# Attention output kept by features, its softmax sums inverted on VectorE, and integers transposed in bfloat16

## The chip, the cores and the metric

One NeuronCore of a Trainium2 chip runs the kernel. The metric is the device time of one execution in microseconds (us). TensorE (PE in the profile) multiplies; its weight loads stand apart as PEld. VectorE (DVE), ScalarE (ACT) and GpSimd (POOL) work on tiles; SyncE (SP) issues most DMAs.

## The reference

Input x has 8 batches of 512 tokens by 256 features. Per batch:

```python
x = layernorm(x * s1)                      # s1, s2: halves of the condition
q, k, v = x @ Wq.T, x @ Wk.T, x @ Wv.T     # each output column scaled (demodulation)
v = v * s2
out = softmax(q k.T / 4) v                 # 16 heads of 16 features
y = (out @ Ww.T) * w_dc + (v @ Wu.T) * u_dc
# int8 feed-forward: rows of y and columns of rhs scaled by their absolute maximum
res = x_in + round(y / s_y) @ round(rhs / s_r) * s_y * s_r
```

## The kernel before

The batches follow one another as t = 0 to 7. One batch is 16 rounds: 4 groups of 4 heads, and 4 tiles of 128 keys each. A round has two units, each of two score products (heads in the lower and the upper 64 rows of the array) and one exponential of 128x1024 on ScalarE (L529). The score banks are double-buffered: unit u waits for the exponential of unit u-2. Two rounds make one of the 8 stretches (`SUPER`) of a batch: `scores_of(r)`, `values_of` of the two rounds before, `scores_of(r+1)`, then `fill(t, i)`, which holds the rest of TensorE's work (L1401 to L1409). In what follows a = t+1 is the batch being prepared, z = t-1 and y = t-2 the batches being finished.

The value product `values_of` (L1037) uses four column groups of 32: 16 columns of a head's values, then ones, so that rows 16 to 31 of each group of 32 hold the softmax sum. Four heads fill `o_acc` (128x512). `save_o` (L537, ScalarE) copies it to `o_t` after each of the four groups of heads, between the exponentials; the next group's values wait for the copy (`o_saved`).

From there the attention output is brought to natural layout and back: `to_natural` (four 128x128 transposes per group of heads), `normalise` on VectorE (L732 inverts the sums, L733 multiplies, into `o_nat`), `to_features` (two times four transposes per batch), `output_features` on VectorE (L748), and the product with the weights, `output` (L1162). VectorE adds the skip and quantises (`quantise`, L760 to L770); TensorE transposes the rounded float32 values (`quantised_transposed`); VectorE subtracts the rounding constant into bfloat16 (`integers`, L774); TensorE multiplies (`int_product`, L1202); VectorE scales (`product`, L790); GpSimd adds the residual (L418) and stores.

The same loop prepares batch a: VectorE multiplies x by the style (`modulate`, L617), measures it (`measure`, L623 to L629) and normalises it; TensorE transposes x; VectorE splits it into a high and a low part (`features`, L610 and L611); TensorE forms q and k (`projected`, L1065); ScalarE copies the high part of each (`high_part`, L513) and VectorE the low part (`low_part`, L650 and L653); DMAs on SP's queue gather both into the stacks. The skip matrix (L1076, "fold"), the norms of q and k for a bound on the scores (`norms`, `largest_norms` L681, `norms_transposed`, `bound_flag`) and the values (L1088) follow. `row_maxima` on TensorE and `row_shift` on VectorE read the flag; with these inputs both take the short branch.

Order and coupling: each engine runs its list in order. `step_fills` writes by hand in which order TensorE's fills claim the three `work` banks; use n waits until use n-3 is freed by its reader, almost always VectorE (`work_freed`), and VectorE takes the banks in the same order (`ready`). VectorE's order is the list at L918 to L986. In it `norms_transposed` of stretch 7 needs `largest_norms(a)`, which stands behind everything that VectorE does for that batch from the fourth low part on:

```python
low_part(a, 3)                 # L963
quantise(z, 0); product(y, 1); normalise(t, 1); skip_matrix(a)
measure(); integers(z, 0); quantise(z, 1)
largest_norms(a); bound_flag(a); v_and_skip(a, 0)
```

TensorE's fills before, in stretches 0 to 7 of a full batch: v1, v2, `to_natural`(z,3) | v3, x transposed twice | `to_features`(z,0), q0, k0 | `to_features`(z,1), `to_natural`(t,0), q1 | integer product (y,0), k1, `output`(z,0) | integer product (y,1), `to_natural`(t,1), fold | `quantised_transposed`(z,0), `output`(z,1), norms | `norms_transposed`, v0 of a, `to_natural`(t,2), `quantised_transposed`(z,1), flag.

After the last value product the rest of batch 7 runs alone: copy, transposes, inverse, transposes, output product, quantisation, integer product, residual, store (L1418 to L1429).

Of the kernel before, what the change touches and what calls it, by code (L numbers as in the profile page):

```python
# [13 lines left out]
P = 128  # L14
# [18 lines left out]
def step_fills(t, last):  # L33

    a, z, y = t + 1, t - 1, t - 2
    if t == 0:
        return [[("row", 0, 0), ("row", 0, 1), ("v", t, 0), ("v", t, 1), ("v", t, 2)],
                [("v", t, 3), ("xt", a, 0), ("xt", a, 1)],
                [("q", a, 0), ("k", a, 0)],
                [("on", t, 0), ("rhs", 0, 0), ("q", a, 1)],  # L40
                [("k", a, 1)],
                [("on", t, 1), ("fold", a, 0), ("rhs", 0, 1)],
                [("norms", a, 0)],
                [("v", a, 0), ("on", t, 2), ("rhs", 0, 2)]]
    if t == last:
        return [[("v", t, 1), ("v", t, 2), ("on", z, 3)],
                [("v", t, 3), ("ot", z, 0), ("ot", z, 1)],
                [("ffn", y, 0), ("y", z, 0)],
                [("ffn", y, 1), ("on", t, 0), ("y", z, 1)],
                [("yqt", z, 0), ("on", t, 1)],  # L50
                [("yqt", z, 1), ("first features", t, 0)],
                [("ffn", z, 0), ("ffn", z, 1), ("y", t, 0), ("y", t, 1)],
                [("on", t, 2)]]
    ffn = [[("ffn", y, n)] if y >= 0 else [] for n in range(2)]
    return [[("v", t, 1), ("v", t, 2), ("on", z, 3)],
            [("v", t, 3), ("xt", a, 0), ("xt", a, 1)],
            [("ot", z, 0), ("q", a, 0), ("k", a, 0)],
            [("ot", z, 1), ("on", t, 0), ("q", a, 1)],
            ffn[0] + [("k", a, 1), ("y", z, 0)],
            ffn[1] + [("on", t, 1), ("fold", a, 0)],  # L60
            [("yqt", z, 0), ("y", z, 1), ("norms", a, 0)],
            [("v", a, 0), ("on", t, 2), ("yqt", z, 1)]]


def adaln_ffn_kernel(nc, x, cond, wq, wk, wv, ww, wu, rhs, out):
# [38 lines left out]
    with ctx:  # L104
# [55 lines left out]
        o_t = sb("o_t", [P, G, S])  # L160
# [7 lines left out]
        inv_den = sb("inv_den", [P, KT, 4])  # L168
        o_nat = sb("o_nat", [P, KT, H])

        o_t2 = sb("o_t2", [P, 2, HC, S // 2])
        y_q = o_t2[:, :, :, :].rearrange("p i c t -> p (i c t)").rearrange("p (k o) -> p k o", k=KT)
# [5 lines left out]
        demod_rows = o_nat[:, :, :].rearrange("p k h -> p (k h)")[0:B, 0:3 * H].rearrange(  # L178
            "b (m o) -> b m o", m=3)
        y_qt = sb("y_qt", [P, HC, S], BF16)  # L180


        by_two = [o_t2[:, :, :, :].rearrange("p m c t -> p (m c t)").rearrange("p (m c i) -> p m c i", m=2, c=HC),
# [1270 lines left out]
```

## Time and profile before

| | us |
|---|---|
| median of 3 runs | 452.48 (452.22 to 453.28) |
| the profiled execution | 452.78 |
| its span, first to last instruction | 451.0 |
| granted TensorE clock, mean | 0.973 of 2.4 GHz |
| busy: PE, DVE, ACT, POOL | 427.1, 245.3, 294.8, 107.2 |

A busy time is a sum over the whole span; it does not tell what waits for what. The chain of waits follows the work that ended last back from its end. The timeline gives each engine's instructions with the idle time before them and what ended it (the releaser). Float32 products on TensorE stand as two records each in the counts. Successive records of an engine can overlap by a few hundredths of a microsecond.

### The profile page before, as it was taken

The numbers are of one execution on the slowest core, as the hardware profiler recorded it, in microseconds if no ns is written. First come the engines' busy times: TensorE is split into PE (matmuls) and PEld (weight loads), VectorE is DVE, ScalarE is ACT, GpSimd is POOL, SyncE is SP. The second block draws the span as 40 slices with busy tenths as digits, with TensorE's granted clock in tenths as the row PEclk, the third lists the DMA queues.
The fourth block names the chain that finished last, engine by engine and source line by source line (L and its number), as shares of the span: only waits on it lengthen the run. The fifth ranks groups of instructions, "written<-read, shape, count | busy, mean of one in ns | idle before, by whom it ended". The sixth has DMA issues, their size and how long they took to land.

```text
span 451.0 us, 7767 instructions
## 1 busy us (share of the span) xinstructions
PE 427.1 (95%) x2700; PEld 238.9 (53%) x2700; DVE 245.3 (54%) x566; ACT 294.8 (65%) x343; POOL 107.2 (24%) x114
## 2 busy tenths in 40 slices
PE   8986999899999999899999999999999999999975
PEld 7773555355545555455544555455545555554444
DVE  6645546544575447644675557654674555537225
ACT  3433488768775787567775776768667776578731
POOL 7176111301130124202340123202330123002201
PEclk9596899999999999999999999999999999999989
DMA  4399179505961299217941499218951399102021
GB/s 155 106 133 135 17 172 137 71 4 156 136 85 55 101 145 152 70 41 157 148 86 55 123 132 156 65 37 163 134 89 56 80 139 146 48 0 95 1 93 47
DMA packets 29326, 44.19 MB, mean 98 GB/s; under 512 B 3880, under 2 KB 15144, under 8 KB 29256
## 3 DMA queue, kind: packets, MB, share of 16 engines
q1 hardware_dynamic: 27040, 38.31, 49.3%
q0 software_dynamic: 1040, 3.70, 2.5%
q10 hardware_dynamic: 1200, 1.59, 2.3%
q8 instruction: 26, 0.43, 0.4%
q14 instruction: 20, 0.16, 0.2%
HBM read 14.17 MB, written 4.25 MB: 41 GB/s over the span
## 4 chain that ended last, share of the span: by engine, by line
PE 84%; DVE 7%; issue 2%; DMA 2%; ACT 2%; SPq 1%; POOL 0%; DVEq 0%; POOLq 0%
PE o_acc L1037 23%; PE scores L1023 16%; PE work L1088 11%; PE work L1065 9%; PE work L1000 8%; PE work L1162 5%; PE work L1076 3%; DMA k_stack<-parts 2%; PE work L1202 2%; ACT probs L529 2%; PE work L1334 1%; PE work L1176 1%; DVE o_t L767 1%; SPq L266 1%; DVE o_t L760 1%
## 5 line engine op out<-in xcount | busy, mean ns | idle before, releaser
L529 ACT ACTIVATE probs<-scores 128x1024 f32<-128x1024 f32 x256 | 247.8, 1024 | 101.7 <-PE scores L1023 101.7
L1037 PE MATMUL o_acc<-probs,v_aug 128*32 128x512 f32 x1024 | 123.3, 598 | 0.2 <-ACT probs L529 0.2
L1023 PE MATMUL scores<-q_stack,k_stack 50*128 50x512 f32 x512 | 95.7, 448 | 7.6 <-ACT probs L529 2.7
L410 POOL TENSOR_TENSOR squares<-parts 128x512 bf16<-128x512 f32 x30 | 31.3, 1042 | 219.3 <-ACT parts L513 219.3
L1023 PEld LDWEIGHTS scores<-q_stack,k_stack 50*128 50x128 f32 x512 | 39.2, 185 | 79.7 <-ACT probs L529 58.7
L1037 PEld LDWEIGHTS o_acc<-probs,v_aug 128*32 128x32 f32 x1024 | 26.6, 109 | 61.6 <-issue 56.7
L1088 PE MATMUL work<-vs_w,x_t 128*128 128x512 f32 x192 | 53.1, 421 | 0.0
L1065 PE MATMUL work<-x_t,qk_w 128*128 128x512 f32 x168 | 44.5, 406 | 0.2 <-DVEq L642 0.2
L1088 PEld LDWEIGHTS work<-vs_w,x_t 128*128 128x128 f32 x192 | 35.9, 197 | 13.4 <-issue 6.1
L671 DVE TENSOR_TENSOR v_aug<-work,rows 128x256 f32<-128x256 f32 x32 | 13.6, 425 | 47.5 <-PE work L1088 47.5
L418 POOL TENSOR_TENSOR res<-res,x_res 128x512 f32<-128x512 f32 x15 | 19.1, 1276 | 74.1 <-DVEq L796 74.1
L1065 PEld LDWEIGHTS work<-x_t,qk_w 128*128 128x128 f32 x168 | 30.0, 188 | 7.1 <-issue 0.6
L1000 PE MATMUL work<-ident,o_t 128*128 128x128 f32 x180 | 26.5, 276 | 0.0
L1162 PE MATMUL work<-w_demod,o_t 128*128 128x256 f32 x112 | 26.5, 379 | 0.0
L1000 PEld LDWEIGHTS work<-ident,o_t 128*128 128x128 f32 x180 | 20.7, 140 | 6.4 <-issue 4.0
L537 ACT ACTIVATE o_t<-o_acc 128x512 f32<-128x512 f32 x32 | 19.2, 599 | 6.1 <-PE o_acc L1037 5.9
L1162 PEld LDWEIGHTS work<-w_demod,o_t 128*128 128x128 f32 x112 | 20.6, 190 | 2.7
L790 DVE SCALAR_TENSOR_TENSOR res<-work,y_scale,rhs_scale_row 128x256 f32<-128x256 f32 x28 | 12.3, 479 | 15.3 <-PE work L1202 15.0
L653 DVE SCALAR_TENSOR_TENSOR parts<-work,cols,parts 128x512 fp32r<-128x512 f32 x14 | 10.5, 750 | 17.7 <-ACT parts L513 17.7
L748 DVE COPY o_t<-work 128x512 f32<-128x512 f32 x14 | 9.7, 692 | 18.6 <-PE work L1000 18.2
L760 DVE TENSOR_TENSOR o_t<-work,skip 128x512 f32<-128x512 f32 x16 | 11.1, 691 | 12.0 <-PE work L1162 8.9
L650 DVE TENSOR_TENSOR parts<-work,parts 128x512 fp32r<-128x512 f32 x14 | 9.7, 692 | 12.4 <-ACT parts L513 12.4
(158 smaller groups left out, 434.5 us busy)
## 6 DMA issues: line engine op xcount, KB each, us to landing
q_stack<-parts SPq DMA_DIRECT2D x96, 128.0 KB, 6.3
k_stack<-parts SPq DMA_DIRECT2D x88, 128.0 KB, 7.7
x_res<-in_x_dram SPq DMA_DIRECT2D x8, 512.0 KB, 4.5
x_sb<-in_x_dram SPq DMA_DIRECT2D x7, 512.0 KB, 3.6
out_dram<-res POOLq DMA_DIRECT2D x7, 512.0 KB, 6.3
rows<-rows_dram SPq DMA_DIRECT2D x7, 384.0 KB, 3.3
rows<-in_cond_dram SPq DMA_DIRECT2D x8, 128.0 KB, 3.7
k_stack<-parts ACTq DMA_DIRECT2D x8, 128.0 KB, 9.9
```

The source lines that it names most:

```text
L410: nc.gpsimd.tensor_tensor(squares[:, n, :], parts[:, n, 0, :], parts[:, n, 0, :], ALU.mult).then_inc(squares_ready, 1)
L418: nc.gpsimd.tensor_tensor(res[:, two, :], res[:, two, :], x_res[:, two, :], ALU.add).then_inc(res_added, 1)
L529: nc.scalar.activation(probs[:, r % RING, pair:pair + 2, :], scores[:, pair:pair + 2, :], ACT.Exp).then_inc(exp_done, 1)
L537: nc.scalar.activation(o_t[:, group % G, :], o_acc[:, :], ACT.Copy).then_inc(o_saved, 1)
L671: nc.vector.tensor_tensor(v_aug[:, k, :, 0:D], both[:, 0:H].rearrange("p (h d) -> p h d", d=D), rows[:, 1, :].rearrange("p (h d) -> p h d" ...
L760: link(nc.vector.tensor_tensor(y, bank.rearrange("p (k o) -> p k o", k=2), skip[:, z % 2, two, :], ALU.add))
L1000: return nc.tensor.transpose(dst, src, ident[0:rows, 0:rows])
L1023: last = nc.tensor.matmul(scores[:, 2 * (u % 2) + e, :], k_stack[top:top + ROWS, t % 2, 2 * g + u % 2, kt * P:(kt + 1) * P], q_stack[top:t ...
L1037: last = nc.tensor.matmul(o_acc[DV * j:DV * (j + 1), :], v_aug[:, kt, 4 * g + j, :], probs[:, r % RING, j, :], start=(kt == 0), stop=(kt = ...
L1065: last = nc.tensor.matmul(bank, lhs, right, start=(n == 0), stop=(n == len(operands) - 1))
L1088: last = nc.tensor.matmul(bank, lhs, right, start=(n == 0), stop=(n == len(operands) - 1))
L1162: last = nc.tensor.matmul(bank[:, k * H:(k + 1) * H], o_t2[:, i, c, k * P:(k + 1) * P], w_demod[:, z % 2, c, :], start=(c == 0), stop=(c = ...
```

## The change

- The value columns of odd groups of heads move to the second 16 of each 32 (`v_aug`, now written by two VectorE instructions), and the heads are regrouped so that the two groups of a pair fill all 128 rows, in the order of the features.
- ScalarE copies the first group of a pair twice, once with a mask for the value rows (`o_raw`) and once for the sum rows (`den`). VectorE adds the second group to both (`add_second`), straight from `o_acc`.
- `invert`: 32x32 block transposition of `den`, two reciprocals, and a block transposition back; `normalise` multiplies 128x512. The result `o_n` is by features, so `output` reads it directly. `to_natural`, `to_features` and `output_features` are gone.
- `quantise` (but for the last batch) writes integers in bfloat16 (`y_int`), which TensorE multiplies by a bfloat16 identity; `integers` clips at -127.
- Fills and VectorE's list are reordered; `quantise` is split into `add_skip` and `quantise`.
- At the end, 12 products of ones by the identity stand in the place of the transposes.

TensorE's fills after: v1, v2 | v3, x transposed twice | q0, k0 | `output`(z,0), `output`(z,1) | q1, k1 | integer product (y,0), fold | integer product (y,1), `quantised_transposed`(z,0), norms | `norms_transposed`, v0 of a, `quantised_transposed`(z,1), flag.

```diff
@@ POOL, start
+            pool.wait_ge(const_ready, 1)
+            nc.gpsimd.tensor_copy(ident_b[:, :], ident[:, :]).then_inc(unit_ready, 1)
@@ ACT
-            def save_o(group):
-                act.wait_ge(pv_done, KT * (group + 1))
-                if group >= G:
-                    act.wait_ge(work_ready, USE[("on", group // G - 1, group % G)] + 1)
-                nc.scalar.activation(o_t[:, group % G, :], o_acc[:, :], ACT.Copy).then_inc(o_saved, 1)
+            def save_first(pair):
+                act.wait_ge(pv_done, KT * (2 * pair + 1))
+                if pair > 0:
+                    act.wait_ge(o_normed, pair)
+                nc.scalar.activation(o_raw[:, :], o_acc[:, :], ACT.Copy, scale=in_half[:, 0:1])
+                nc.scalar.activation(den[:, :], o_acc[:, :], ACT.Copy, scale=in_half[:, 1:2]).then_inc(o_saved, 1)
...
-                    if i == 0 and t > 0:
-                        save_o(t * G - 1)
-                    if i in (2, 4, 6):
-                        save_o(t * G + i // 2 - 1)
+                    if i in (2, 6):
+                        save_first(2 * t + i // 4)
...
-                        if i == 3:
+                        if i == 4:
                             high_part(a, 2)
-                        if i == 4:
                             high_part(a, 3)
@@ DVE, v_and_skip
-                nc.vector.tensor_tensor(v_aug[:, k, :, 0:D], both[:, 0:H].rearrange("p (h d) -> p h d", d=D),
-                                        rows[:, 1, :].rearrange("p (h d) -> p h d", d=D), ALU.mult)
+                by_pair = "p (n j e d) -> p n j e d"
+                for e in range(2):
+                    nc.vector.tensor_tensor(
+                        v_aug[:, k, :, e * D:(e + 1) * D].rearrange("p (n e j) d -> p n e j d", e=2, j=4)[:, :, e, :, :],
+                        both[:, 0:H].rearrange(by_pair, e=2, j=4, d=D)[:, :, :, e, :],
+                        rows[:, 1, :].rearrange(by_pair, e=2, j=4, d=D)[:, :, :, e, :], ALU.mult)
@@ DVE, in place of normalise(z, g), first_chunk and output_features
+            def add_second(pair):
+                dve.wait_ge(pv_done, KT * (2 * pair + 2))
+                dve.wait_ge(o_saved, 2 * pair + 1)
+                nc.vector.scalar_tensor_tensor(den[:, :], o_acc[:, :], in_half[:, 0:1], den[:, :], ALU.mult, ALU.add
+                                               ).then_inc(den_ready, 1)
+                nc.vector.scalar_tensor_tensor(o_raw[:, :], o_acc[:, :], in_half[:, 1:2], o_raw[:, :], ALU.mult, ALU.add
+                                               ).then_inc(o_saved, 1)
+            def invert(pair):
+                dve.wait_ge(den_ready, pair + 1)
+                link(nc.vector.transpose(den_t[:, :], den[:, :]))
+                by_half = den_t[:, :].rearrange("p (b e d) -> p b e d", e=2, d=D)
+                for e in range(2):
+                    last = nc.vector.reciprocal(inv_den[:, :, 1 - e], by_half[:, :, e, 0])
+                link(last)
+                link(nc.vector.transpose(inv_t[:, :].rearrange("p (b e d) -> p b e d", e=2, d=D),
+                                         inv_den[:, :, :].unsqueeze(3).broadcast_to([P, S // DV, 2, D])))
+            def normalise(pair):
+                dve.wait_ge(o_saved, 2 * pair + 2)
+                if pair < 2 * B - 1:
+                    nc.vector.tensor_tensor(o_n[:, pair % 2, :], o_raw[:, :], inv_t[:, :], ALU.mult).then_inc(o_normed, 1)
+                else:
+                    for i in range(2):
+                        tokens = slice(i * HALF_S, (i + 1) * HALF_S)
+                        nc.vector.tensor_tensor(o_n[:, pair % 2, tokens], o_raw[:, tokens], inv_t[:, tokens], ALU.mult
+                                                ).then_inc(last_normed, 1)
@@ DVE, quantise
+                if z < B - 1:
+                    for k in range(2):
+                        last = nc.vector.tensor_scalar(y_q[:, 2 * i + k, :], y[:, k, :], y_inv[:, 2 * i + k:2 * i + k + 1],
+                                                       MAGIC, ALU.mult, ALU.add)
+                    link(last)
+                    nc.vector.tensor_scalar(y_int[:, two, :], y, MAGIC, INT8_MAX, ALU.subtract, ALU.min
+                                            ).then_inc(yq_ready, 1)
+                    return
@@ DVE, start
+            for e in range(2):
+                link(nc.vector.tensor_reduce(in_half[:, e:e + 1], ident[:, :].rearrange("p (j e d) -> p j e d", e=2, d=D)[:, :, e, :],
+                                             AX.XY, ALU.add))
+            dve.sem_inc(half_ready, 1)
@@ PE, quantised_transposed
-                    transpose_pair(claim("yqt", z, i), y_q, i, work_ready)
+                    bank = claim("yqt", z, i)
+                    for c in range(HC):
+                        for k in range(2):
+                            last = nc.tensor.matmul(bank[:, (2 * c + k) * P:(2 * c + k + 1) * P],
+                                                    y_int[:, 2 * i + k, c * P:(c + 1) * P], ident_b[:, :],
+                                                    start=True, stop=True)
+                    last.then_inc(work_ready, 1)
@@ PE, end
-            to_natural(z, 3)
-            pe.wait_ge(on_ready, z * G + G)
-            one_chunk(scores[:, 1, :], 1).then_inc(features_t, 1)
+            keep_clock(scores[:, 0, :], 12)
```

VectorE's list for a full batch, after the change:

```python
add_second(2*z + 1); v_and_skip(t, 1); v_and_skip(t, 2)
invert(2*z + 1); normalise(2*z + 1); v_and_skip(t, 3)
features(a, 0); features(a, 1); low_part(a, 0); low_part(a, 1)
add_skip(z, 0); add_skip(z, 1); add_second(2*t); low_part(a, 2); low_part(a, 3)
invert(2*t); normalise(2*t); quantise(z, 0); product(y, 0); skip_matrix(a)
modulate(a + 1); measure(); quantise(z, 1); product(y, 1); integers(z, 0)
largest_norms(a); bound_flag(a); v_and_skip(a, 0); integers(z, 1)
row_shift(a); normalise_x(a + 1)
```

## Rows read from the trace of the kernel before

**Rows 1.** Part 1 of the page: busy us (share of the span) xinstructions
```profile
PE 427.1 (95%) x2700; PEld 238.9 (53%) x2700; DVE 245.3 (54%) x566; ACT 294.8 (65%) x343; POOL 107.2 (24%) x114
```

**Rows 2.** Chain of waits, 225 to 240 us: start, duration, what
```profile
225.42 0.66 PE scores L1023 x4
226.08 1.85 PE o_acc L1037 x16
...
229.19 1.74 PE work L1162 x8
...
230.95 0.70 DVE o_t L760
...
236.94 0.87 PE work L1000 x8
```

**Rows 3.** TensorE's timeline: start, duration, operation [idle before, releaser]
```profile
216.15 1.64 PE L1065 MATMUL work<-x_t,qk_w 128*128 128x512 f32 x6
...
235.21 0.27 PE L1000 MATMUL work<-ident,norm_max 128*1 128x128 f32 x1 [0.78 <-DVE norm_max L681]
...
253.62 0.65 PE L1000 MATMUL work<-ident,o_nat 128*128 128x128 f32 x4
```

**Rows 4.** Windows: length, busy (instructions) by engine, clock, DMA, GB/s
```profile
88.65:137.98 49.33, 48.17 (x309) 25.66 (x310) 27.38 (x65) 35.25 (x40) 8.48 (x9) 1.00 0.54 88
188.12:238.16 50.04, 48.91 (x317) 26.34 (x318) 29.16 (x67) 35.35 (x40) 11.84 (x12) 1.00 0.59 107
338.17:387.54 49.37, 48.93 (x317) 26.34 (x318) 25.43 (x57) 35.34 (x40) 8.93 (x9) 1.00 0.59 96
387.54:433.06 45.52, 44.49 (x302) 21.35 (x302) 18.70 (x44) 32.77 (x36) 6.62 (x6) 1.00 0.18 59
```

**Rows 5.** Groups by line and form: busy us, mean ns, idle before
```profile
L1202 PE MATMUL work<-rhs_q,y_qt 128*128 128x256 bf16 x56 | 8.4, 275 | 0.0
...
L732 DVE RECIPROCAL inv_den<-work 128x16 f32<-128x16 f32 x31 | 8.0, 258 | 14.6 <-PE work L1000 9.4 <-DVE res L790 1.5 <-DVE o_t L748 1.5
```

**Rows 6.** VectorE's timeline, a full batch
```profile
214.48 1.23 DVE L617 TENSOR_TENSOR x_sb<-x_sb,rows 128x1024 f32<-128x1024 f32 x1 [0.22 <-DVE parts L653]
...
218.54 0.69 DVE L650 TENSOR_TENSOR parts<-work,parts 128x512 fp32r<-128x512 f32 x1 [1.12 <-ACT parts L513]
...
220.40 0.69 DVE L763 TENSOR_REDUCE amax<-o_t 128x2 f32<-128x512 f32 x1 [0.15 <-DVE o_t L760]
...
222.18 0.43 DVE L770 TENSOR_SCALAR o_t<-o_t 128x512 f32<-128x512 f32 x1
223.29 0.88 DVE L790 SCALAR_TENSOR_TENSOR res<-work,y_scale,rhs_scale_row 128x256 f32<-128x256 f32 x2 [0.68 <-PE work L1202]
...
227.12 1.41 DVE L623 BATCH_NORM_STATS2 stats<-x_sb 128x6 f32<-128x256 f32 x4 [0.24 <-DVE vs_w L611]
...
229.22 0.69 DVE L774 TENSOR_SCALAR y_qt<-work 128x512 bf16<-128x512 f32 x1
...
249.66 0.43 DVE L671 TENSOR_TENSOR v_aug<-work,rows 128x256 f32<-128x256 f32 x1 [3.59 <-PE work L1088]
...
252.95 0.69 DVE L611 TENSOR_TENSOR x_t<-work,x_t 128x512 fp32r<-128x512 f32 x1
```

**Rows 7.** Chain of waits, 430 to 440 us
```profile
433.08 0.61 ACT o_t L537
...
436.38 3.52 PE work L1176 x8
```

**Rows 8.** ScalarE's timeline, batch 7
```profile
419.12 3.77 ACT L529 ACTIVATE probs<-scores 128x1024 f32<-128x1024 f32 x4 [1.04 <-PE scores L1023]
```

**Rows 9.** Windows around idle TensorE; the clock stands behind POOL's time
```profile
34.00:36.00 2.00, 0.06 (x1) 0.00 (x0) 1.20 (x2) 0.04 (x1) 2.00 (x2) 1.00 1.08 128
36.00:38.00 2.00, 0.73 (x4) 0.33 (x4) 0.58 (x2) 0.87 (x1) 2.00 (x1) 0.83 1.05 125
...
437.00:439.00 2.00, 2.00 (x6) 1.55 (x6) 0.74 (x2) 0.00 (x0) 0.00 (x0) 0.50 0.00 0
```

More of the change, by code:

```diff
@@ L966, in _ @@
                 if y >= 0:
-                    product(y, 1)
-                normalise(t, 1)
+                    product(y, 0)
                 skip_matrix(a)
@@ L972, in _ @@
                 if a + 1 < B:
+                    modulate(a + 1)
                     measure()
                 if z >= 0:
+                    quantise(z, 1)
+                if y >= 0:
+                    product(y, 1)
+                if z >= 0:
                     integers(z, 0)
-                    quantise(z, 1)
                 largest_norms(a)
@@ L979, in _ @@
                 v_and_skip(a, 0)
-                normalise(t, 2)
                 if t == 0:
@@ L987, in _ @@
                     normalise_x(a + 1)
-            normalise(B - 1, 3)
-            quantise(B - 1, 0)
-            quantise(B - 1, 1)
+            add_second(2 * B - 1)
+            invert(2 * B - 1)
+            normalise(2 * B - 1)
+            for i in range(2):
+                add_skip(B - 1, i)
+                quantise(B - 1, i)
             product(B - 1, 0)
@@ L1130, in row_maxima @@
                 pe.nop()
-            def to_natural(z, g):
-                pe.wait_ge(o_saved, z * G + g + 1)
-                if (z, g) == (B - 1, G - 1):
-                    bank, done = scores[:, 0, :], natural_t
-                else:
-                    bank, done = claim("on", z, g), work_ready
-                for q in range(KT):
-                    last = transpose(bank[:, q * P:(q + 1) * P], o_t[:, g, q * P:(q + 1) * P])
-                last.then_inc(done, 1)
             def transpose_pair(bank, src, i, done):
@@ L1300, in fill @@
                         int_product(z, 1)
+                    else:
+                        if y >= 0:
+                            int_product(y, 1)
+                        if not first:
+                            quantised_transposed(z, 0)
+                        norms(a)
+                else:
+                    if last:
                         last_output(t, 0, 0)
@@ L1303, in fill @@
                     else:
-                        if not first:
-                            quantised_transposed(z, 0)
-                            output(z, 1)
-                        norms(a)
-                else:
-                    if last:
-                        to_natural(t, 2)
-                    else:
                         norms_transposed(a)
                         values(a, 0)
-                        to_natural(t, 2)
                         if first:
```

218 lines of the change are left out of this document (91 added, 127 removed).

## The prediction

> **What bounds the kernel now.** I read the busy shares first: TensorE is busy 95% of the span, ScalarE 65%, VectorE 54% [rows 1]. That says that TensorE's work counts, not that it alone sets the time. So I read the chain that ended last through a batch [rows 2]: it runs along TensorE (scores, values, fills), and behind the last output product (229.19) it leaves it for VectorE, where the skip is added at 230.95. It comes back with `norms_transposed` at 235.21, for which TensorE had idled 0.78 us, released by `norm_max` [rows 3]. One VectorE chain per batch is thus already on the path.
>
> Then the batches by stretches between their first score products [rows 4]. Call them 0 to 7: batch 1 takes 49.33 us, batches 2 to 5 50.05 each (137.98 to 338.17), batch 6 49.37, batch 7 45.52 up to the last value product. The granted clock is 1.00 in all. I cut a full batch at two points. A: from its first scores (188.12) to the end of the second k projection (216.15 + 1.64 = 217.8) [rows 3], 29.7. B: from there over VectorE to `norms_transposed`, 235.2, 17.4. C: to the next batch's scores, 238.16, 2.95.
>
> **A, TensorE's part.** Eight transposes take 0.87 in the chain [rows 2], so a group of four is 0.44. The change takes four such groups out of A (two of `to_natural`, two of `to_features`): 1.76. The integer product moves behind the k projection: 8.4 us for 14 of them is 0.6 [rows 5]. Both output products now stand ahead of it, 1.74 each [rows 2]: +3.5. One wait is new. The last `v_and_skip` starts at 249.66 and the second low part of x ends at 252.95 + 0.69 = 253.64 [rows 6], while TensorE was free at 253.62 and covered the hand-over with transposes [rows 3]. Those are gone, and `v_and_skip` has one instruction more (about 0.13), so the q projection waits some 0.35. A becomes 29.7 - 1.8 - 0.6 + 3.5 + 0.35 = 31.1.
>
> **B, VectorE's part, in the new order.** `low_part(3)` ends 1.43 after the k projection (217.80 to 218.54 + 0.69) [rows 6]; with 0.22 for the semaphores behind it, 1.65. Everything after it is now queued back to back:
> - `invert` and `normalise`. The block transpose is in no row. Bounds: 0.43, the cheapest 128x512 float32 SBUF step (222.18), and 1.23, the 128x1024 one (214.48). I take 0.69, what plain 128x512 steps take (229.22) [rows 6], since it moves 512 elements a row once. Two reciprocals of 16 columns at 0.26 [rows 5] overlap to 0.45, links 0.1, the multiplication 0.69: 0.69 x 2 + 0.45 + 0.1 + 0.69 = 2.6.
> - `quantise(0)` without its addition: 220.40 to 222.61, 2.2. `product(0)`: 0.88 and a link of 0.24, 1.1. `skip_matrix`: two of 0.69 and links, 1.65.
> - `modulate`, moved in from where it was hidden: 1.25. `measure`: 227.12 to 229.22, 2.1 [rows 6].
> - `quantise(1)` 2.2, `product(1)` 1.1, `integers` 0.9, the reduction 0.7.
>
> Sum: 1.65 + 2.6 + 2.2 + 1.1 + 1.65 + 1.25 + 2.1 + 2.2 + 1.1 + 0.9 + 0.7 = 17.5. It was 17.4: the two additions left, and so did waits for TensorE inside, but the inversion, `modulate` and one product came in.
>
> TensorE no longer has work for that time. Two of its eight stretches a batch lie there, then the scores and values of a third: 0.66 + 1.85 + 0.66 = 3.2 [rows 2]. The first stretch adds a product (0.6) and the fold, which like an output product is eight matrix passes of 256 columns (1.7): 5.5. The second adds only 1.3, so ScalarE stretches it to about 5.5: two copies of 0.6 [rows 7] stand between its exponentials. TensorE is at `norms_transposed` 5.5 + 5.5 + 3.2 = 14.2 us after the k projection and waits 3.2, where it waited 0.8. What transposes are saved behind A is thus worth nothing.
>
> **C.** 2.95, less a group of four transposes (0.44) and about 0.1 for the bfloat16 ones: 2.4. A full batch: 31.1 + 17.5 + 2.4 = 51.0, +0.95.
>
> Here I weigh a page. The Trainium skill (VectorE: DVE Perf Modes, The three transpose paths) gives 311 ns for a VectorE transposition of 128x128 bfloat16, in 32x32 blocks only. An estimate by four such pieces is 1.24 us an instruction, so 1.1 more for each `invert`; a full batch would be 52.1 by its chain alone. No row here shows one.
>
> **The sum.** Start and batch 0: two more reductions ahead of a VectorE memset and one more POOL copy, +0.2 (nothing to 0.8, since VectorE idles later anyway); two of batch 0's stretches lose their transposes or a projection, and ScalarE's exponentials and copies set them, while others keep their length: +0.9. Batch 1 has no integer products, so B is 15.3: 48.8, -0.5. Batches 2 to 5: +0.95 x 4 = +3.8. Batch 6 has no `modulate` or `measure` and B would be 14.1, so TensorE's 14.2 takes its place: 47.7, -1.6. Batch 7: fewer transposes, but ScalarE gives 3.77 of exponentials and idles 1.04 a stretch there already [rows 8], 4.8, and now holds most stretches: -0.5. Tail: from the last copy of values to the output products 3.3 us (433.08 to 436.38 [rows 7]); now two additions (1.45), the inversion (1.95) and half a multiplication, 3.95: +0.6. If the added fillers keep the clock up, the cold output products (3.52) get back 0.9 of that on the path: +0.1, between -0.3 and +0.6. Total +2.4: the profiled execution's 452.8 us becomes 455.2; the median of the runs stands 0.3 under it, 454.9.
>
> **The clock.** At 34 to 36 us TensorE is busy 0.06 of 2 us, and in the next 2 us the granted clock falls; at 437 to 439, behind the tail's copies, it is 0.50 (1.2 GHz) [rows 9]. The new wait of 3.2 looks like these, though it lies between dense stretches. In the tail the cold output products take 3.52 [rows 7] for what takes 1.74 hot, so a fall costs some 1.6 us. I take one in batches 2 to 5: 456.5. The Trainium skill (TensorE: Matmul & The Clock Gate, HAM oscillation) tells of a kernel whose bursts are parted by waits and that turns cold behind each. By that rule every full batch would pay.
>
> **Rivals.**
> - *Each long wait cools TensorE.* By the rows [rows 9], 4 x 1.6 = 6.4 us on 454.9, 461.3. Against it: batch 7's waits for ScalarE [rows 8] brought no fall, its clock is 1.00. 0.16.
> - *The chain is shorter (faster).* It decides where B falls below 16.85, 0.65 less than I sum: five batches then take 3.3 back, the 2.4 and 0.9 more. Two transposes at 0.43 give 0.5; if reciprocals and links overlap and q's wait vanishes too, 1.0 a batch: 454.9 - 5 = 450. The releaser of `norms_transposed` would stay VectorE. 0.24.
> - *TensorE stays the bound, as six groups of transposes a batch suggest.* 2.6 + 0.2 + the 0.8 wait is 3.6; over 7 batches 25, less some 6 that ScalarE's stretches give back: 434. It needs B under 14.2, against a sum of 17.5. 0.05.
> - *The transposition takes 1.2 us.* `invert` then also delays the last `v_and_skip`, where its slack is only 0.2 us, and so q: 6 x 2 more, 467. 0.06.
>
> **Numbers.** My forecast, the VectorE chain with a batch of 51 us, has 0.49; its own range is 451.5 to 459.5 (B half a microsecond either way in five batches, none to two falls), the likeliest time 456.5. Below 449.5 lies about 0.1, above 463 about 0.1. A measurement of this kernel tells 0.2%, 0.9 us, from no change. Faster: the shorter chain and the TensorE case, 0.29. Same: a part of the forecast near 452.5, 0.13. Slower: the rest, 0.58.
>
> **What would show it.** After the change: TensorE idle before `norms_transposed`, released by `norm_max`, about 3 us in batches 2 to 5, 1.5 in batch 1, near nothing in batch 6 (wrong if it is under 1 in the full ones). VectorE without a gap between the fourth low part and `norm_max`, 16 us. Batches of 51.0, 48.8 and 47.7. The transposition at 0.6 to 0.75. A granted clock under 1.00 behind one of the waits. TensorE's busy time down by some 20 us and the span not. The prediction is wrong at its root if the chain of waits never passes over VectorE between the projections and the norms.

## The result, and the profile after

The changed kernel takes 468.76 us (median of 4 runs, 466.3 to 470.45), the kernel before 452.35 beside it: a ratio of 1.036, with a 95% interval of 1.033 to 1.039. The prediction said 456.5, with an own range of 451.5 to 459.5 and about 0.1 each for below 449.5 and above 463: the sign came true, the time lies outside both. The profiled execution took 470.2 us, 17.4 more than that of before, and the spans differ by as much (468.4 and 451.0).

The page after, busy time and the groups that matter; the chain's shares before were PE 84%, DVE 7%:

```profile
PE 416.7 (89%) x2532; PEld 218.8 (47%) x2532; DVE 273.8 (58%) x634; ACT 294.5 (63%) x341; POOL 107.3 (23%) x115
...
PE 57%; DVE 26%; issue 6%; DMA 4%; ACT 3%; SPq 2%; DVEq 0%; ACTq 0%
...
L1032 PE MATMUL work<-ident,norm_max 128*1 128x128 f32 x8 | 2.2, 281 | 15.7 <-DVE norm_max L689 15.7
```

TensorE was busy 10 us less [rows 1], where the prediction had some 20, and it idles more than that, 15.7 us of it for `norm_max`. A quarter of the chain is VectorE's.

The batches by windows, in the columns of [rows 4]; the first line is batch 1, then 2, 3, 5 and 6:

```profile
90.70:141.01 50.31, 46.12 (x285) 22.95 (x286) 31.04 (x71) 35.36 (x40) 8.72 (x9) 0.98 0.54 86
141.01:195.17 54.16, 48.75 (x293) 24.03 (x294) 32.78 (x76) 35.36 (x40) 9.55 (x10) 0.95 0.56 99
195.17:247.07 51.90, 46.92 (x294) 23.70 (x294) 32.28 (x76) 35.35 (x40) 11.96 (x13) 0.98 0.60 104
301.25:353.10 51.85, 47.13 (x293) 23.85 (x294) 31.85 (x75) 35.35 (x40) 11.67 (x13) 0.98 0.57 104
353.10:404.39 51.29, 48.43 (x293) 23.81 (x294) 29.97 (x66) 35.35 (x40) 11.01 (x12) 0.96 0.55 92
```

There are two kinds of full batch: 54.2 us (2 and 4) and 51.9 (3 and 5). Cut at the prediction's points, in us:

| batch | A | B | C | length | predicted | excess over before |
|---|---|---|---|---|---|---|
| start and 0 | | | | 90.70 | 89.75 | +2.05 |
| 1 | 31.40 | 15.90 | 3.01 | 50.31 | 48.8 | +0.98 |
| 2 | 33.78 | 17.24 | 3.14 | 54.16 | 51.0 | |
| 3 | 31.42 | 17.24 | 3.24 | 51.90 | 51.0 | |
| 4 | 33.66 | 17.25 | 3.27 | 54.18 | 51.0 | |
| 5 | 31.41 | 17.24 | 3.20 | 51.85 | 51.0 | +11.9 (2 to 5) |
| 6 | 33.59 | 14.12 | 3.58 | 51.29 | 47.7 | +1.92 |
| 7 and tail | | | | 64.01 | 63.1 | +0.55 |

The column on the right sums to the 17.4. Part B is the forecast's chain. VectorE's timeline of batch 3, the end of the fourth low part to the flag, answers to [rows 6]:

```profile
227.33 0.69 DVE L654 TENSOR_TENSOR parts<-work,parts 128x512 fp32r<-128x512 f32 x1 [0.55 <-ACT parts L524]
228.17 0.71 DVE L742 STREAM_TRANSPOSE den_t<-den 128x512 f32<-128x512 f32 x1
228.91 0.36 DVE L745 RECIPROCAL inv_den<-den_t 128x16 f32<-128x16 f32 x2
229.31 0.71 DVE L747 STREAM_TRANSPOSE inv_t<-inv_den 128x512 f32<-128x512 f32 x1
230.06 0.69 DVE L756 TENSOR_TENSOR o_n<-o_raw,inv_t 128x512 f32<-128x512 f32 x1
...
235.62 1.23 DVE L621 TENSOR_TENSOR x_sb<-x_sb,rows 128x1024 f32<-128x1024 f32 x1 [0.32 <-DVE vs_w L615]
236.88 1.41 DVE L627 BATCH_NORM_STATS2 stats<-x_sb 128x6 f32<-128x256 f32 x4
...
243.08 0.69 DVE L689 TENSOR_REDUCE norm_max<-work 128x1 f32<-128x512 f32 x1 [0.24 <-DVE y_qt L798]
...
244.95 0.14 DVE L703 TENSOR_SCALAR flag<-bound 1x1 int32<-1x1 f32 x1
```

No idle time over 0.32 us stands between 227.33 and `norm_max`. TensorE's timeline of the same stretch answers to [rows 3]:

```profile
236.86 0.50 PE L1057 MATMUL scores<-q_stack,k_stack 50*128 50x512 f32 x2 [0.54 <-ACT probs L540]
...
240.05 0.73 PE L1057 MATMUL scores<-q_stack,k_stack 50*128 50x512 f32 x4
243.83 0.27 PE L1032 MATMUL work<-ident,norm_max 128*1 128x128 f32 x1 [3.04 <-DVE norm_max L689]
243.93 1.95 PE L1122 MATMUL work<-vs_w,x_t 128*128 128x512 f32 x6
245.69 0.65 PE L1211 MATMUL work<-ident_b,y_int 128*128 128x128 bf16 x4
247.07 1.22 PE L1057 MATMUL scores<-q_stack,k_stack 50*128 50x512 f32 x4 [0.73 <-SPq L284]
```

TensorE runs dry for 3.04 us; after that its products are slow (scores 1.22 for 0.73), and it idles again before the next scores. Windows over this wait, and the last two lines over the wait of batch 4, which looks the same; the clock stands behind POOL's time:

```profile
241.00:242.00 1.00, 0.00 (x0) 0.00 (x0) 0.90 (x3) 1.00 (x2) 0.00 (x0) 1.00 0.00 0
245.00:246.00 1.00, 1.00 (x6) 0.47 (x5) 0.17 (x2) 0.00 (x0) 1.00 (x2) 0.53 0.64 225
248.00:250.00 2.00, 2.00 (x14) 0.47 (x16) 0.67 (x3) 1.84 (x2) 1.09 (x2) 0.50 0.62 187
...
295.00:296.00 1.00, 0.00 (x0) 0.00 (x0) 1.00 (x3) 1.00 (x2) 0.00 (x0) 1.00 0.00 0
298.00:300.00 2.00, 1.95 (x11) 1.32 (x11) 0.99 (x6) 0.00 (x0) 1.83 (x2) 1.00 0.24 84
```

From 245 to some 252 us the clock is at 0.50, the lower of the two levels (1.2 GHz), and A of batch 4 is 2.24 us longer than A of batch 3. After the equally long wait of batch 4 it stays at 1.00.

So two things were not in the sum: C did not fall below 3 in batches 1 to 6, and there were clock falls at 84, 139, 245, 350 and 405 us, where the kernel before has none between batch 0 (up to 48 us) and the tail. The first eight runs below separate VectorE's queue, the flag behind C, and the falls; the last four try the rest.

### The profile page after: what moved, and what is told of

Read it like the earlier page. It is cut to its first block, busy times and chain, and to the rows that moved or that the text cites. A ratio compares the mean times of both kernels' runs of the same rounds, so it can differ in the third digit from the quotient of the medians.

```text
span 468.4 us, 7377 instructions
## 1 busy us (share of the span) xinstructions
PE 416.7 (89%) x2532; PEld 218.8 (47%) x2532; DVE 273.8 (58%) x634; ACT 294.5 (63%) x341; POOL 107.3 (23%) x115
## 4 chain that ended last, share of the span: by engine, by line
PE 57%; DVE 26%; issue 6%; DMA 4%; ACT 3%; SPq 2%; DVEq 0%; ACTq 0%
PE o_acc L1071 17%; PE scores L1057 11%; PE work L1122 9%; PE work L1099 9%; PE work L1182 5%; ACT probs L540 2%; DMA k_stack<-parts 2%; DVE x_t L615 2%; DVE x_t L614 2%; DVE amax L778 2%; DVE res L814 2%; DVE y_q L783 2%; DVE stats L627 2%; DMA y_q<-in_L_cond_k_weight_dram 1%; DVE x_sb L621 1%
## 5 line engine op out<-in xcount | busy, mean ns | idle before, releaser
L1071 PE MATMUL o_acc<-probs,v_aug 128*32 128x512 f32 x1024 | 130.6, 630 | 0.0
L1057 PE MATMUL scores<-q_stack,k_stack 50*128 50x512 f32 x512 | 100.2, 461 | 22.3 <-ACT probs L540 11.7
L1122 PEld LDWEIGHTS work<-vs_w,x_t 128*128 128x128 f32 x192 | 36.4, 199 | 13.5 <-issue 6.2
L677 DVE TENSOR_TENSOR v_aug<-work,rows 128x128 f32<-128x128 f32 x64 | 15.6, 286 | 29.5 <-PE work L1122 29.5
L770 DVE TENSOR_TENSOR y_q<-work,skip 128x512 f32<-128x512 f32 x16 | 11.1, 691 | 36.6 <-PE work L1182 35.7
L733 DVE SCALAR_TENSOR_TENSOR den<-o_acc,in_half,den 128x512 f32<-128x512 f32 x16 | 12.0, 749 | 25.3 <-PE o_acc L1071 25.3
L1182 PE MATMUL work<-w_demod,o_n 128*128 128x256 f32 x112 | 26.3, 386 | 0.0
L1182 PEld LDWEIGHTS work<-w_demod,o_n 128*128 128x128 f32 x112 | 20.6, 190 | 5.4 <-issue 2.9
L638 DVE TENSOR_SCALAR x_sb<-x_sb,mv,rstd 128x256 f32<-128x256 f32 x32 | 11.4, 417 | 9.5 <-issue 9.3
L1032 PE MATMUL work<-ident,norm_max 128*1 128x128 f32 x8 | 2.2, 281 | 15.7 <-DVE norm_max L689 15.7
L1110 PE MATMUL work<-wu_t,wv_scaled 128*128 128x256 f32 x64 | 15.4, 384 | 0.0
L405 POOL TENSOR_SCALAR wv_scaled<-wv_nat,cols 128x256 f32<-128x256 f32 x16 | 14.8, 933 | 0.1
```

Of the source, the lines that this page charges most:

```text
L405: last = nc.gpsimd.tensor_scalar(wv_scaled[:, c, :], wv_nat[:, c, :], cols[:, a, 2 + c:3 + c], None, ALU.mult)
L677: nc.vector.tensor_tensor(v_aug[:, k, :, e * D:(e + 1) * D].rearrange("p (n e j) d -> p n e j d", e=2, j=4)[:, :, e, :, :], both[:, 0:H].r ...
L1057: last = nc.tensor.matmul(scores[:, 2 * (u % 2) + e, :], k_stack[top:top + ROWS, t % 2, head, kt * P:(kt + 1) * P], q_stack[top:top + ROWS ...
L1071: last = nc.tensor.matmul(o_acc[DV * j:DV * (j + 1), :], v_aug[:, kt, 4 * g + j, :], probs[:, r % RING, 2 * (j % 2) + j // 2, :], start=(k ...
L1110: last = nc.tensor.matmul(bank[:, hc * H:(hc + 1) * H], wv_scaled[:, c, hc * P:(hc + 1) * P], wu_t[:, c, :], start=(c == 0), stop=(c == HC ...
L1122: last = nc.tensor.matmul(bank, lhs, right, start=(n == 0), stop=(n == len(operands) - 1))
```

## The experiments

All of them are edits of the changed kernel unless it says otherwise. The flag is 1 where the scores are so small that no shift by row maxima is wanted; TensorE, VectorE and SyncE each read it from SBUF and branch.

**e1: SyncE doesn't read the flag.** Left out: SyncE's branch for large scores.

```diff
-                wait(flag_ready, a + 1)
-                small = sp.value_load(flag[0:1, 0:1], min_val=0, max_val=1)
-                with sp.If(small == 1):
-                    sp.sem_inc(shift_loaded, SHIFT)
...
+                sp.sem_inc(shift_loaded, SHIFT)
```

> The changed kernel, but SyncE adds to shift_loaded without reading the flag, so its branch for large scores is left out. The after trace has 3.2 us from norms_transposed to the next batch's scores, and the scores there wait for SyncE (SPq), which reads the flag 1.3 us after norms_transposed. If SyncE's reading of the flag is a hand-over on the path, this stretch falls to TensorE's own work, about 2.4 us, in batches 1 to 5 and from 3.6 in batch 6: 468.8 us becomes about 463. If VectorE's chain alone sets the batch, the stretch and the time stay (468 to 469). B (k projection to norms_transposed) stays 17.2 either way.

467.08 us, ratio 1.033 (1.029 to 1.036). C stayed at 3.2 to 3.7. Where the wait before the scores had been put down to SyncE, it now reads "issue" (1.76 in batch 6). That SyncE holds the scores is refuted, although the profile names it. The falls moved (they stand at all five long waits).

**e2: filler products in the wait.** Eight of 128 columns (four in batch 1) go ahead of `norms`, which moves one stretch later.

```diff
+                        if not first and t < B - 2:
+                            keep_clock(claim("norms", a, 0), 4 if t == 1 else 8)
+                            norms(a)
                         norms_transposed(a)
```

> The changed kernel with products of ones by the identity (8 calls, some 1.9 us, in batches 2 to 5, 4 in batch 1) and then the norms product in the place where TensorE waits 3.0 us before norms_transposed. VectorE's chain is untouched, so B stays 17.2. If the clock falls come from that wait, the scores and values of batches 2, 4 and 6 go back from 1.22 and 3.6 us to 0.73 and 1.9, each fall gives 2.3 us back, and the time is about 460 to 462. If the falls come from elsewhere (the end of batch 0, the start), it stays at 466 to 469.

467.41 us, ratio 1.033 (1.027 to 1.038). The fillers did their part: the wait is 0.80, and no fall follows it any more. But the time hardly moved, and the 460 to 462 did not come. Full batches without a fall take 51.8 to 52.4, for 51.9 in the changed kernel, since VectorE's chain sets them, and falls came elsewhere. TensorE's timeline and a window in batch 4 of e2 show another place:

```profile
288.74 0.50 PE L1057 MATMUL scores<-q_stack,k_stack 50*128 50x512 f32 x2 [0.87 <-ACT probs L540]
289.65 0.50 PE L1057 MATMUL scores<-q_stack,k_stack 50*128 50x512 f32 x2 [0.41 <-ACT probs L540]
290.07 3.39 PE L1071 MATMUL o_acc<-probs,v_aug 128*32 128x512 f32 x16
...
297.41 0.27 PE L1032 MATMUL work<-ident,norm_max 128*1 128x128 f32 x1 [0.80 <-DVE norm_max L689]
```
```profile
290.00:294.00 4.00, 4.00 (x22) 1.07 (x20) 3.46 (x14) 1.42 (x2) 0.00 (x0) 0.57 0.13 15
```

Two short waits for ScalarE in stretch 6, then values in 3.39 for 1.92 at a lower clock. Falls stood at 85, 133, 290 and 403 us.

**e3: measurement early.** For all batches but the first, `modulate` and `measure` go ahead of the output additions on VectorE, where they were hidden before.

```diff
                 low_part(a, 1)
+                if t > 0 and a + 1 < B:
+                    modulate(a + 1)
+                    measure()
                 if z >= 0:
...
-                if a + 1 < B:
+                if t == 0:
                     modulate(a + 1)
```

> The changed kernel with modulate and measure of batches from 2 on moved out of B, ahead of add_skip, where VectorE idles. If VectorE's queue between the last k projection and the norms is the cause, B falls by 3.35 from 17.2 to about 14.2 (TensorE's own arrival), the 3.0 us wait goes, and with it the clock falls; full batches take 31.4 + 14.2 + 3.2 = 48.8 us and the whole about 449, under the kernel before. If the block transposes or the masks are what costs, B stays over 16 and the time over 460. If only the clock is at fault, the gain is 7 to 9 us at most.

452.69 us over 10 runs, ratio 1.001 (0.998 to 1.003). Five changed lines, all of order, give back the whole 16 us. TensorE's timeline in e3:

```profile
232.82 0.73 PE L1060 MATMUL scores<-q_stack,k_stack 50*128 50x512 f32 x4
233.49 0.27 PE L1035 MATMUL work<-ident,norm_max 128*1 128x128 f32 x1
233.51 1.65 PE L1125 MATMUL work<-vs_w,x_t 128*128 128x512 f32 x6
235.00 0.40 PE L1214 MATMUL work<-ident_b,y_int 128*128 128x128 bf16 x4
237.08 0.75 PE L1060 MATMUL scores<-q_stack,k_stack 50*128 50x512 f32 x4 [1.68 <-SPq L284]
```

B is 14.13 (17.24) and the wait for `norm_max` is gone: VectorE's queue was the bound. It is the forecast's "TensorE's 14.2". But C is 3.5 to 3.6 with 1.68 idle, and two falls remain in the full batches (237 and 288 us), each behind such an idle; A is 33.0 behind them, 1.6 more than elsewhere. With these the 449 expected was missed.

**e4: e3, and SyncE doesn't read the flag** (the edit of e1, the same part left out).

> Both: measure early and no reading of the flag on SyncE. If the two costs are separate and add up, full batches take 31.4 + 14.2 + 2.4 = 48.0 us and the whole is about 444. If the flag's hand-over only showed because the chain was late, this is no faster than the kernel with measure early alone.

452.86 us over 10 runs, ratio 0.999 (0.997 to 1.002), nothing gained on e3. C is 3.49 to 3.59 in the full batches, its idle 1.6 to 1.7 again, now all "issue". In the profile the flag's instruction ends at 235.28 and the scores start at 237.61: 2.33 us, of which the profile gives the idle part to no other engine.

**e6: e3 without any reading of the flag.** Left out: on all three engines, the branch for large scores.

```diff
-                pe.wait_ge(flag_ready, a + 1)
-                pe.sem_inc(spare, 1)
-                small = pe.value_load(flag[0:1, 0:1], min_val=0, max_val=1)
-                with pe.If(small == 1):
-                    pe.sem_inc(m_ready, M_USES)
...
+                pe.sem_inc(m_ready, M_USES)
```

> Measure early, and no engine reads the flag (the branch for large scores is left out on SyncE, TensorE and VectorE). In the run with SyncE alone freed the scores still came 3.5 us behind norms_transposed, idle for 1.6 to 1.7 with no releaser but TensorE's own issue. If that is TensorE's wait for the flag and its read, the stretch falls to 2.1 us, full batches to 47.7, falls of the clock in batches 3 and 4 go, and the time is about 442. If something else holds the scores (a stack, a semaphore of SyncE), it stays at 452.

439.15 us, ratio 0.970 (0.967 to 0.972), 13.5 less than e3. TensorE's timeline, the same place as in e3:

```profile
229.60 1.65 PE L1094 MATMUL work<-vs_w,x_t 128*128 128x512 f32 x6
231.09 0.40 PE L1161 MATMUL work<-ident_b,y_int 128*128 128x128 bf16 x4
231.41 0.74 PE L1029 MATMUL scores<-q_stack,k_stack 50*128 50x512 f32 x4
```

C is 1.84, without idle: the flag's route costs 1.6 to 1.8 in batches 2 to 6, 1.2 in batch 1 and 0.7 in batch 0, 10.4 in all. The rest of the gain is near the two falls of e3, 3.3. Between batch 0 and the tail one fall is left (407 us), and full batches take 47.4, one 47.7. In this execution, the falls went with the idle.

**e9: the kernel before, without any reading of the flag** (the same part left out).

> The kernel before, with no engine reading the flag (the branch for large scores is left out). TensorE's idle in front of a batch's first scores is 0.35 us there (the transposes cover the rest), so if the flag costs only what idles, about 0.4 x 7 = 2.5 us go: 450. If the branch costs TensorE 1.3 us a batch whatever is queued, as in the changed kernel, it falls to 444. Either way this is what the same kernel without flags (439, with measure early) has to be set against.

450.33 us, ratio 0.995 (0.993 to 0.997). TensorE's timeline:

```profile
234.44 0.27 PE L969 MATMUL work<-ident,norm_max 128*1 128x128 f32 x1 [0.78 <-DVE norm_max L669]
234.54 1.63 PE L1057 MATMUL work<-vs_w,x_t 128*128 128x512 f32 x6
236.02 1.03 PE L969 MATMUL work<-ident,o_t 128*128 128x128 f32 x8
236.98 0.73 PE L992 MATMUL scores<-q_stack,k_stack 50*128 50x512 f32 x4
```

C is 2.54, against 2.95. In the kernel before, the flag thus cost 0.4 a batch: the eight transposes (1.03 us) ran beside it. Without the flag, C goes from 2.54 to 1.84 with the change: 0.70, near the 0.54 that I had taken. e6 against e9, 439.15 against 450.33, compares the change with `measure` early to the kernel before, both without the flag. It is no price of the change alone: in e9 TensorE still waits 0.78 a full batch for `norm_max`, some 4 us in all, and no run tried whether another order on VectorE gives these back in the kernel before. The same holds where e5 and e7 below are set against the kernel before.

**e12: e3 with six float32 transposes ahead of the flag**, about what the change took out there.

```diff
+            def transposes_again(bank, n):
+                for q in range(n):
+                    transpose(bank[:, q % KT * P:(q % KT + 1) * P], ident[:, :])
...
+                            transposes_again(claim("yqt", z, 1), 6)
                             quantised_transposed(z, 1)
```

> This is e3 (measurement early) with six float32 128x128 transposes ahead of the bfloat16 ones in stretch 7, batches 2 to 7 of the preparation: by the rows of before (eight in 1.03) about 0.65 us more of TensorE's work between norms_transposed and the next scores, which is what the change took out there. It tells what the transposes before did for the flag. Theory 'covered': reading the flag and branching is a time of its own that runs beside TensorE's queued work; then C stays at e3's 3.5 to 3.6, TensorE's idle time before the scores falls from 1.7 to about 1.0, and the whole stays at 452 to 454 us. Rival 'queue': the flag's route starts behind the work issued ahead of it; then C grows to 4.1 to 4.2 with the idle time unchanged, 456 to 457 us. Rival 'before's order was quicker by itself': with as much work as before, C falls to 2.95 as in the kernel before, 449 to 450 us.

448.83 us, ratio 0.991 (0.988 to 0.993), so faster than e3 with more work. TensorE's timeline:

```profile
235.77 0.27 PE L1035 MATMUL work<-ident,norm_max 128*1 128x128 f32 x1
235.79 1.63 PE L1125 MATMUL work<-vs_w,x_t 128*128 128x512 f32 x6
237.26 0.82 PE L1035 MATMUL work<-ident 128*128 128x128 f32 x6
237.92 0.39 PE L1218 MATMUL work<-ident_b,y_int 128*128 128x128 bf16 x4
239.39 0.73 PE L1060 MATMUL scores<-q_stack,k_stack 50*128 50x512 f32 x4 [1.09 <-SPq L284]
```

C is 3.49 to 3.62 as in e3, and its idle fell from 1.68 to 1.09: the transposes cost nothing, they lie beside the flag's route, as "covered" had it. The total is under what that theory said (452 to 454). In the profiled execution no fall followed the shorter idle, which is worth e3's 3.3 us, but one came at 133 us, and the start was longer; this execution, the slowest of the four, is only 0.9 under the profiled one of e3 (450.99 and 451.89). For the other runs only the mean clock speaks: 0.972 to 0.981 in e12, 0.964 to 0.971 in the ten runs of e3, so fewer or shorter falls. The third theory's time came true by another way than its own, since its C of 2.95 did not.

**e10: the changed kernel without any reading of the flag** (the same part left out).

> The changed kernel as it is, with no engine reading the flag and nothing else moved. B stays 17.2 and the wait before norms_transposed 3.0; the stretch behind it falls from 3.0 to 3.6 to about 1.9, so full batches are 50.6, batch 6 49.4 less a fall, and the time about 460, with the clock's falls still there as the 3.0 us wait is. If the falls need both idle stretches together, they go too and it is about 455.

462.54 us, ratio 1.022 (1.019 to 1.026). The wait for `norm_max` is as long as ever (3.05, once 3.41), and the clock falls at every one of the five (137, 188, 240, 294 and 345 us). TensorE's timeline of batch 3, where C has no idle but slow products:

```profile
241.21 0.37 PE L1001 MATMUL work<-ident,norm_max 128*1 128x128 f32 x1 [3.06 <-DVE norm_max L677]
...
244.59 1.22 PE L1026 MATMUL scores<-q_stack,k_stack 50*128 50x512 f32 x4
```

With a fall C lasts 2.85 to 3.38, since its products run cold; in batch 6, where none comes, 1.91. Without the flag, the waits alone bring the falls. The flag is worth 6.2 us here, less than in e6, since the falls take a part of C back.

**e8: eight float32 transposes a batch put back into B** (four before the fold, four before the second integer product).

> The changed kernel with eight 128x128 float32 transposes a batch put back on TensorE, of ones and zeros, four ahead of the fold and four ahead of the second integer product. They are 0.9 us of work a batch. If TensorE's saved work behind the last k projection is worth nothing, the wait before norms_transposed shrinks from 3.0 to about 2.1 to 2.5 and the time stays at 466 to 469, or falls where the shorter wait avoids falls of the clock. If TensorE is still the bound, it rises by 0.9 x 7 to about 475.

467.78 us, ratio 1.035 (1.032 to 1.038), the changed kernel's own time. The wait for `norm_max` is 2.61 instead of 3.05, B 17.25 as before. Work taken from TensorE in B is worth nothing in the full batches; in batch 6, where TensorE is the bound, B grows from 14.12 to 14.57.

**e11: integers transposed in float32 again**, the bfloat16 part of the change undone.

```diff
-                                             ready("yqt", z, i).rearrange("p (c t) -> p c t", c=HC), -INT8_MAX, None,
-                                             ALU.max))
+                                             ready("yqt", z, i).rearrange("p (c t) -> p c t", c=HC), MAGIC, None,
+                                             ALU.subtract))
...
+                    transpose_pair(claim("yqt", z, i), y_q, i, work_ready)
```

> The changed kernel with the integers of all batches again transposed in float32 (quantise with clip, minimum and addition; four transposes; integers subtracts the constant), all else as changed. VectorE's steps are as many and as long, and TensorE's 0.1 to 0.2 us a group lies under its waits, so the time stays within the spread of the changed kernel, 465 to 470. If the bfloat16 products are what lets the clock fall, or what delays the flag, it falls to under 462.

466.49 us, ratio 1.032 (1.029 to 1.035), within the changed kernel's spread. A gain or loss of the bfloat16 part can't be measured in this version.

**e5: norms early.** e3, and the squares' sums go into stretch 5, `norms_transposed` into stretch 6, with `largest_norms` and the flag's instructions moved ahead on VectorE, and `quantise(z, 1)` behind them.

```diff
-            ffn[0] + [("fold", a, 0)],
-            ffn[1] + [("yqt", z, 0), ("norms", a, 0)],
+            ffn[0] + [("fold", a, 0), ("norms", a, 0)],
+            ffn[1] + [("yqt", z, 0)],
...
                     quantise(z, 0)
+                    largest_norms(a)
...
+                bound_flag(a)
```

> Measure early as before, and the norms product moved to the end of stretch 5, its transposition to stretch 6, largest_norms behind quantise(0) and the flag ahead of product(1). With the flag known some 4 us before TensorE reads it, the 3.5 us between norms_transposed and the next scores, of which 1.7 were idle for the flag, shrink; the stretch from the k projection to the next scores falls from 17.7 to about 16.5, full batches from 49.1 to about 47.9, and the time to about 444, clearly under the kernel before. If TensorE's branch costs its time wherever the flag stands (an instruction fetch, not the flag), it stays near 49 us a batch and 452.

446.76 us, ratio 0.987 (0.985 to 0.990): faster than both kernels, with everything computed, though not the 444 expected. Full batches without a fall take 48.5 to 48.6. TensorE's timeline:

```profile
226.91 0.27 PE L1036 MATMUL work<-ident,norm_max 128*1 128x128 f32 x1
...
228.62 0.50 PE L1061 MATMUL scores<-q_stack,k_stack 50*128 50x512 f32 x2 [0.71 <-ACT probs L540]
...
235.20 0.73 PE L1061 MATMUL scores<-q_stack,k_stack 50*128 50x512 f32 x4 [0.81 <-issue]
```

The flag is written by 228.53, over 6 us ahead of the scores, and still 0.81 of idle is left there. So there is a part of the flag's route that starts only when TensorE's sequencer comes to it.

**e7: e5, and the second output product in stretch 6**, where TensorE waits for ScalarE. `o_n` gets a third buffer, for which the demodulation's tiles are laid over `y_qt`. VectorE's addition and quantisation of that half move behind it.

```diff
-            [("y", z, 0), ("y", z, 1)],
+            [("y", z, 0)],
...
-            ffn[1] + [("yqt", z, 0)],
+            ffn[1] + [("yqt", z, 0), ("y", z, 1)],
...
-        o_n = sb("o_n", [P, 2, S])
+        o_n = sb("o_n", [P, 3, S])
```

> As the kernel with norms early, and the second output product of a batch moved from stretch 3 to stretch 6 (o_n for the even pair held twice), where ScalarE's two copies leave TensorE idle. If TensorE is the bound with ScalarE holding stretch 6 at 5.5 us, batches fall by another 0.7 to 1.1, to about 47, and fewer clock falls: 437 to 440. If VectorE's queue binds again (its addition and quantisation now come late), batches stay at 48 or rise.

443.01 us, ratio 0.979 (0.977 to 0.981), the fastest version with everything computed: 9.6 us under the kernel before (452.63 beside it) and 25.8 under the change. Full batches take 47.9, one 50.4 with a fall at 187 us. The wait in stretch 6 is gone, but before the next scores 1.17 is idle for "issue", more than in e5, which is why the 437 to 440 were not reached.

## Why the prediction was wrong, and where it was right

**Right: the bound, and B.** B was to be 17.5 and is 17.24; the wait for `norm_max` 3.2 and is 3.04 to 3.06 in batches 2 to 5, 1.5 in batch 1 and is 2.04, near nothing in batch 6 and is none. The chain of waits passes over VectorE (26% of it), as the prediction wanted. A was to be 31.1 and is 31.4 where the clock stays up. The transposition, bounded by 0.43 and 1.23 and taken at 0.69, measures 0.71; by the group after the change:

```profile
L747 DVE STREAM_TRANSPOSE inv_t<-inv_den 128x512 f32<-128x512 f32 x16 | 11.4, 711 | 0.5
```

My estimate by a figure of the Trainium skill (VectorE: DVE Perf Modes, The three transpose paths), four pieces of 311 ns or 1.24 us, is refuted for this shape. "What transposes are saved behind A is worth nothing": e8 shows it. And e3 shows the cause by undoing it: with `modulate` and `measure` back where they were hidden, B is 14.13, the 14.2 that the prediction gave TensorE, and the 16 us are gone.

**Wrong, first step: "C. 2.95, less a group of four transposes (0.44) and about 0.1 for the bfloat16 ones: 2.4."** C measured 3.0 to 3.6. I had cut TensorE's work out of a stretch without asking what waited beside it. The route of the flag (VectorE's three small steps, then the reading and the branch on TensorE) ran under the transposes; the profile of before showed it only as 0.4 us of "issue" ahead of the scores. e9 prices it there at 0.4 a batch, e6 after the change at 1.7, and e12 shows transposes put back at no cost. The 1.7 that e6 takes out of e3's C of some 3.55 has three parts: 0.4 was paid before (2.95 against 2.54), 0.7 is the work that covered it (2.54 against 1.84), and 0.6 is that the flag's route itself became longer (3.55 against 2.95). Only the second is shown to be the lost cover; why the route is longer stays open. By the table C is over the forecast by 0.8 in each full batch, 0.6 in batch 1 and 1.2 in batch 6, 5 us in all.

**Wrong, second step: "I take one in batches 2 to 5", at 1.6 us.** In the profiled execution three such falls came in A (batches 2, 4 and 6), of 2.2 to 2.4 each (33.6 to 33.8 against 31.4), 7 us, and two more at the end of batch 0 and the start of batch 7. The price of 1.6 was taken from products in the tail; here a fall lasts some 7 us from 245, over scores and values too. Number and price both failed, and 2.3 is no constant either: in e3 and e4 a fall costs A 1.6, in e10 and e11 0.7 to 1.2 behind most waits, with a part more in C. The rival "each long wait cools TensorE", at 0.16, was nearer than the forecast, but had the wrong set: in this execution the waits of batches 1, 3 and 5 brought a fall and those of 2 and 4 none, in e1, e10 and e11 every wait did, and in e2 and e3 falls followed short idles of stretch 6 (0.87 and 0.41) and the flag's 1.7. The Trainium skill's rule (TensorE: Matmul & The Clock Gate, HAM oscillation), that bursts parted by waits turn cold behind each, agrees with e1, e10 and e11 and not with this execution. That the kernel's spread of 4 us comes from the number of falls is not shown: its two slower runs (470.23 and 470.45) have the higher mean clocks, 0.955 and 0.956, and the two faster ones 0.947 and 0.950.

**Smaller ones.** A is 0.3 a batch longer than summed, 1.8 over six batches; B is 0.5 less in all (0.26 less in four batches, 0.6 more in batch 1). With C's 5.0, the falls' 6.8, and 0.95 each at the start and at the end, this is the 15.0 by which the profiled execution (+17.4) exceeds the sum without a fall (+2.4). The copies on ScalarE took 0.69, not 0.60:

```profile
L548 ACT ACTIVATE o_raw<-o_acc,in_half 128x512 f32<-128x512 f32 x16 | 11.0, 688 | 3.0 <-PE o_acc L1071 3.0
```

Start and batch 0 came to +2.05 for +1.1; a fall at 84 us lies in it, behind idles of 1.30 and 0.42 for ScalarE in stretch 6, but I didn't take it apart. Batch 6 was to gain 1.6 and lost 1.92: the fall, 2.2, and C, 1.2, make up 3.4 of the 3.5. TensorE's busy time fell by 10.4, not by some 20: its values and scores, as many as before, took 130.6 and 100.2 us for 123.3 and 95.7, 11.8 more, which the falls fit (scores in 1.22 for 0.73).

**What stays open.** What makes one wait bring a fall and the next, equally long one none. Whether the kernel before gains by an order of its own. Then why the flag's route is longer after the change (2.33 us in e4 from the flag's last instruction to the scores; before, 236.46 to 238.16, 1.70): e12 put the work back and C did not return to 2.95. And how the route divides between the semaphore, the reading and the branch; no run took them singly.

## What to carry to other kernels

Before counting removed work as gain, list for that stretch what else is under way beside it, small control steps too: a branch on a value from SBUF, of which the profile shows only an "issue" of 0.4 us, cost 1.7 in e3, with its cover gone and its route longer. When an engine's queue becomes the path, first move what isn't due out of it (five lines, 16 us here), then move work of the starved engine into its gaps, and only then look at savings. In a dense kernel on TensorE a new wait of a few us should be priced with a clock fall of some 1 to 2.4 us behind it, as an even chance at least: three of five waits brought one in the profiled execution, all five in e1, e10 and e11.

## What the hardware showed that I had not expected

- The clock can fall behind short idles in otherwise dense work: a wait of 2.04 us (batch 1), 1.7 (e3), even 0.87 and 0.41 with two score products between (e2). It is back at 1.00 some 3 to 7 us later. Equally long waits of 3.04 to 3.06 us bring a fall or none.
- Reading a flag and branching on TensorE takes far more than an instruction: 2.33 us from the flag's end to the next scores (e4), of which 1.68 are idle, and 0.81 of idle even with the flag written over 6 us ahead (e5). The Trainium skill prices a compare-and-branch at about 108 ns (Advanced Engine Details and Errata, Control Flow Timing); no run here takes that instruction singly. The Trainium skill also says that a taken branch can wait for its target to be fetched by DMA (Runtime: NRT & Kernel Launch, Instruction fetch mechanics). The traces don't bear it out here: the profile's DMA queues show no instruction packet between `norms_transposed` and the scores, in e3, in e4 or in the changed kernel; in e3 one of 16 KB starts 0.2 to 0.5 us behind the scores in batches 2 to 7. The queues of e3 at 233.5 to 237.1, and at 237.1 to 239 (scores at 237.08):

```profile
q0 software_dynamic: 144, 0.52, 41.8%
...
q8 instruction: 1, 0.02, 4.4%
```

- The releaser that the profile names was not the one: "SPq L284" stood before the scores, and with SyncE's wait removed (e1, e4) they started no earlier.
